# Last layer of a four-layer kernel: another hand order of its stages on all engines, and a rearranged opening

## The chip, the cores and the metric

One Trainium2 chip, one of its cores. The metric is the device time of one launch in microseconds (us). The time before is 2538.4 us, the median of three runs (2533.71 to 2541.52).

## What is computed

Four sub-layers run one after another on a batch of 2 sequences of 2048 tokens with 256 channels; each adds its result to its input. The change touches the last two, which the kernel does together. Per row of tokens, with `x` the sum of the layers so far:

```python
h = layernorm(x)                                   # without weights
xn = layernorm(h) * ln_w + ln_b
u, v, base = split(silu(xn @ uv_w.T + uv_b))       # 512, 512, 128 columns
q, k = rope(base * gamma[0] + beta[0]), rope(base * gamma[1] + beta[1])
kern = square(relu(q @ k.T / sqrt(128) + w[j - i + 127]))   # 2048 x 2048 for each sequence
y = x + (u * (kern @ v)) @ o_w.T + o_b + h
out = y + layernorm(y) @ (ternary(weight) * alpha) + d_bias
```

The kernel treats a whole sequence of 2048 tokens as the attention's length: 16 tiles of 128 keys by 4 chunks of 512 queries, for each of 2 sequences.

## The kernel before, in words

Layer functions `layer_a`, `layer_b` and `layer_c` run in turn, with all engines meeting between them. The change is in `layer_c` alone (from line 1787 on). It has two kinds of work.

**Steps.** There are 16 steps of 256 tokens (`n` from 0 to 15, eight for each sequence). In a step GpSimd (POOL) adds the two halves of the input (`sum`, L2016) when its rows have come by DMA (`load`, SyncE's queue, which waits until the sum before is done); VectorE (DVE) takes the moments (`moments`, L2150 to L2156); POOL takes the root (`moments`, L2020); DVE normalizes (`norm`, L2166); TensorE (PE) turns the rows (`turn_h`, L2342); ScalarE (ACT) and DVE split the result in a high and a low part (`turn_h`, L2076 and L2204), since each product is made of three matmuls (`product3`, lines L39 to L41). PE then makes `base` (6 matmuls of 256 columns), `u` in two halves (12 each) and `v` in two halves (7 of 512 columns each, the first one the bias, L2374). For `base`, ACT applies silu and scales (L2084 to L2093), DVE multiplies by the rotary table (L2211), POOL adds (L2033), and ACT and DVE split (`qk`, L2122 and L2222).

**Tiles.** There are 128 tiles (`i`). For each PE makes `scores` (3 matmuls of 512 columns), DVE turns them to `kern` in two instructions (L2232 reads the bank, L2236), ACT takes the high part (`high`, L2126), POOL the low part (`low`, L2037), and PE multiplies with `v` (`values`, 12 matmuls of 512 columns). After every 16 tiles a chunk is finished by stages that hang on later tiles (`after`): gate, project, residual, `turn_y`, `ternary`, `out`.

Steps 0 to 7 open the layer and overlap with tiles 0 to 9; steps 8 to 15 lie beside tiles 48 to 63. In the rest there are tiles alone.

**The order is written out by hand.** `order` names for each engine the stages of one slot and a shift; `turns` and `in_slots` unroll it. Each engine executes its own list strictly in that order, so an instruction that waits holds all that stand behind it in the list.

**PSUM banks.** `bank_uses` walks PE's list and gives each use the next bank: of all eight until the first `scores`, from then on of four (`narrow`: 0, 1, 2, 7) for everything but the outputs of `values`. A bank's next user waits on PE (`wait_bank`) until the engine that reads the last one has drained it. In the list before, with eight narrow uses to a slot, `turn_h(n+1)` follows a half of `u` in its bank; the bank of `scores` 2k is the one of `base`.

**Opening.** `shifts` on PE (20 records of one column, L2323, and 4 of 512 columns, L2328) makes the sums of the weights with `ln_b`; it is issued behind `turn_h` of step 0. DVE's `shifts` (L2180 to L2187) makes bias rows of them, which `base` on ACT and `v` on PE wait for. DVE's `weights` (L2173) makes the low part of the weights. After `v` (1, 1) PE makes `total` (L2335), one sum that DVE's `signs` (L2192 to L2200, after `qk` of step 1) waits for in its middle. `scores` of tile 0 need `q_lo_ready` of 2, that is `qk` of steps 0 and 1.

The two lists around the first steps, as the tables unroll them (numbers are step, or step and half, or tile):

```
PE before   turn_h0 [shifts] base0 u0,0 u0,1 v0,0 turn_h1 v0,1 base1 u1,0 u1,1 v1,0 turn_h2 v1,1 [total]
            base2 u2,0 u2,1 v2,0 scores0 turn_h3 scores1 v2,1 base3 u3,0 u3,1 v3,0 scores2 values0 turn_h4
DVE before  moments0 norm0 [weights] turn_h0 [shifts] moments1 norm1 base0 turn_h1 moments2 qk0 norm2 base1
            turn_h2 moments3 qk1 [signs] norm3 base2 turn_h3 kern0 kern1 v0,0 moments4 qk2 norm4 base3
```

Of the kernel before, what the change touches and what calls it, by code (L numbers as in the profile page):

```python
# [10 lines left out]
ALU = mybir.AluOpType  # L11
ACT = mybir.ActivationFunctionType
# [4 lines left out]
KC = D // P  # L17
# [1769 lines left out]
def layer_c(nc, io, psum, sem, early):  # L1787
# [9 lines left out]
    narrow, outputs = (0, 1, 2, 7), (3, 4, 5, 6)  # L1797

    order = {
        "act": [("v", 1, 2), ("base", 0, 3), ("u", 0, 3), ("after", 0, 4), ("high", 1, 3), ("u", 1, 3), ("turn_h", 0, 4),  # L1800
                ("v", 0, 3), ("high", 0, 4), ("qk", 0, 3), ("after", 1, 4)],
        "pe": [("u", 0, 3), ("u", 1, 3), ("after", 1, 2), ("v", 0, 3), ("scores", 0, 4), ("values", 0, 3),
               ("turn_h", 0, 4), ("scores", 1, 4), ("values", 1, 3), ("after", 0, 3), ("v", 1, 3), ("base", 0, 4)],
        "dve": [("norm", 0, 5), ("base", 0, 4), ("v", 1, 1), ("after", 0, 5), ("turn_h", 0, 5), ("kern", 0, 5),
                ("kern", 1, 5), ("v", 0, 2), ("moments", 0, 6), ("qk", 0, 4), ("after", 1, 5)],
        "sp": [("tile", 1, -1), ("tile", 0, 0), ("store_u", 0, 0), ("load", 0, 4), ("residual", 0, 1), ("rope", 0, 1)],
        "pool": [("after", 0, 7), ("sum", 0, 8), ("base", 0, 6), ("residual", 0, 7), ("low", 0, 7), ("after", 1, 7),
                 ("moments", 0, 8), ("low", 1, 7)],
    }
    of_tiles = ("values", "scores", "kern", "high", "low", "after", "tile")  # L1810
    halved = ("u", "v")
# [9 lines left out]

    def bank_uses():
        slot_banks = tuple(range(8))
        for name, slot, part in turns(order["pe"], slots):
            for at in places(name, part, slot):
                if name == "scores":
                    slot_banks = narrow
                if name == "values":
                    if at[0] % NT == 0:
                        for e in range(C_EC):  # L1830
                            yield ("o", (at[0] // NT, e)), outputs
                elif name == "after":
                    if NT <= at[0] and at[0] % NT in project_after:
                        stage, n = project_after[at[0] % NT]
                        yield (stage, (at[0] // NT - 1, n)), slot_banks
                else:
                    yield (name, at if name in halved else at[0]), slot_banks
                    if name == "turn_h" and at[0] == 0:
                        yield ("shifts", 0), slot_banks
                        yield ("shifts", 1), slot_banks  # L1840
                    if (name, at) == ("v", (1, 1)):
                        yield ("total", 0), slot_banks
        for stage, n in project_after.values():
            yield (stage, (C_TILES // NT - 1, n)), slot_banks

    with ExitStack() as ctx:
# [26 lines left out]
        x2 = [sb(f"x2{k}", [P, 2, D]) for k in range(2)]  # L1873
# [126 lines left out]
        @block.gpsimd  # L2000
        def _(pool):
            pool.memset(power[:], -0.5).then_inc(consts_ready, 1)
            pool.memset(ones[:], 1.0).then_inc(consts_ready, 1)
            pool.memset(e0[:].bitcast(F32), 0.0).then_inc(consts_ready, 1)
            pool.wait_ge(consts_ready, 3)
            pool.memset(e0[0:1, :].bitcast(F32), 1.0).then_inc(consts_ready, 1)
            pool.memset(e0[32:33, :].bitcast(F32), 1.0).then_inc(consts_ready, 1)
            pool.wait_ge(consts_ready, 5)

            def sum_(n):  # L2010
                if n > 0:
                    pool.wait_ge(x_loaded, 32 * n)
                if n > 1:
                    pool.wait_ge(xn_ready, n - 1)
                    pool.wait_ge(r_ready, n - 1)
                pool.tensor_tensor(x2[n % 2][:], x_in[:], y_in[:], ALU.add).then_inc(summed, 1)  # L2016

            def moments(n):
                pool.wait_ge(var_ready, n + 1)
                pool.tensor_tensor(rstd[:], var[:], power[:].rearrange("p (a b) -> p a b", a=2), ALU.pow).then_inc(rstd_ready, 1)  # L2020

            def residual(n):
                pool.wait_ge(xn_ready, n + 1)
                if n == 0:
                    pool.wait_ge(row_in, 80)
                r = r_out[n % 2]
                pool.tensor_tensor(r[:], x2[n % 2][:], r[:], ALU.add).then_inc(pool_own, 1)
                pool.wait_ge(pool_own, n + 1)
                pool.tensor_tensor(r[:], r[:], o_b[:, None, :].broadcast_to([P, 2, D]), ALU.add).then_inc(r_ready, 1)

            def base_(n):
                pool.wait_ge(rotated, n + 1)
                pool.tensor_tensor(turned[:, :, 0, :], turned[:, :, 0, :], turned[:, :, 1, :], ALU.add).then_inc(turned_ready, 1)  # L2033

            def low_part(i):
                pool.wait_ge(hi_ready, i + 1)
                pool.tensor_tensor(kern_lo[i % RING][:], kern[i % RING][:], kern_hi[i % RING][:].bitcast(F32), ALU.subtract)\  # L2037
                    .then_inc(lo_ready, 1)

            def add_bias(g):  # L2040
                pool.wait_ge(x3_ready, 2 * g + 2)
                if g > 0:
                    pool.wait_ge(stored, 16 * g)
                pool.tensor_tensor(x_out[:], x3[:], d_bias[:, None, :].broadcast_to([P, 4, D]), ALU.add).then_inc(biased, 1)

            def root(g):
                pool.wait_ge(y_var_ready, g + 1)
                pool.tensor_tensor(y_rstd[:], y_var[:], power[:], ALU.pow).then_inc(y_rstd_ready, 1)

            def after(i):  # L2050
                if i >= NT and i % NT == 5:
                    add_bias(i // NT - 1)
                if i >= NT and i % NT == 6:
                    root(i // NT - 1)

            in_slots(order["pool"], slots, places, {"low": low_part, "after": after, "base": base_, "moments": moments,
                                                    "residual": residual, "sum": sum_})
            root(C_TILES // NT - 1)
            add_bias(C_TILES // NT - 1)

        @block.scalar
        def _(act):
# [5 lines left out]
                act.activation(shift_rows[:, c, :], ones[:], ACT.Copy, scale=gb[:, 1, c:c + 1]).then_inc(rows_ready, 1)  # L2068
            for c in range(KC):
                act.activation(w_hi[:, c, :], w_raw[:, c, :], ACT.Copy, scale=gb[:, 0, c:c + 1]).then_inc(w_hi_ready, 1)  # L2070

            def turn_h(n):
                ring.wait_full(act, ("turn_h", n))
# [69 lines left out]
        def _(dve):  # L2143
            own = Links(dve, dve_own)
            dve.wait_ge(consts_ready, 5)

            def moments(n):
                dve.wait_ge(summed, n + 1)
                for w in range(2):
                    ins = dve.bn_stats(stats[:, w, :], x2[n % 2][:, w, :])  # L2150
                own.link(ins)
                for w in range(2):
                    ins = dve.bn_aggr(mv[:, w, :], stats[:, w, :])
                own.link(ins)
                dve.tensor_scalar(var[:, :, 0], mv[:, :, 1], EPS, None, ALU.add)
                dve.tensor_scalar(var[:, :, 1], mv[:, :, 1], 1.0 + EPS, EPS * EPS, ALU.mult, ALU.add).then_inc(var_ready, 1)  # L2156
# [156 lines left out]

        @block.tensor
        def _(pe):
            pe.wait_ge(consts_ready, 5)

            def shifts():
                pe.wait_ge(rows_ready, KC)
                ring.wait_bank(pe, ("shifts", 0))  # L2320
                for n, col in enumerate(list(range(0, C_E, P)) + [2 * C_E]):
                    for c in range(KC):
                        ins = pe.matmul(ring.out(("shifts", 0), C_EC + 1)[:, n:n + 1], w_raw[:, c, col:col + P], gb[:, 1, c:c + 1],  # L2323
                                        start=(c == 0), stop=(c == KC - 1))
                ring.written(ins, ("shifts", 0))
                ring.wait_bank(pe, ("shifts", 1))
                for c in range(KC):
                    ins = pe.matmul(ring.out(("shifts", 1), C_E), shift_rows[:, c, :], w_raw[:, c, C_E:2 * C_E],  # L2328
                                    start=(c == 0), stop=(c == KC - 1))
                ring.written(ins, ("shifts", 1))  # L2330

            def total_():
                pe.wait_ge(dve_setup, 1)
# [3 lines left out]
            def turn_h(n):  # L2337
# [4 lines left out]
                        ins = pe.transpose(ring.out(("turn_h", n), 512)[:, c * C_STEP + w * P:c * C_STEP + (w + 1) * P],  # L2342
                                           xn[:, w, c * P:(c + 1) * P], ident[:])
                ring.written(ins, ("turn_h", n))
                if n == 0:
                    shifts()

            def columns(n, job, part, col):
                for c in range(KC):
# [18 lines left out]
            def v(n, w):  # L2368
                at = n, w
                if n == 0 and w == 0:  # L2370
                    pe.wait_ge(b_ready, 4)
                ring.wait_bank(pe, ("v", at))
                tok = slice(w * P, (w + 1) * P)
                pe.matmul(ring.out(("v", at), C_E), e0[:], b_rows[:], start=True, stop=False)  # L2374
# [219 lines left out]
```

## Time and profile before

| | |
|---|---|
| profiled execution, whole | 2539.21 us |
| its span, first to last instruction | 2537.1 us |
| mean granted TensorE clock | 0.972 of full |
| PE busy | 2433.2 us (96%) |
| DVE busy | 1979.4 us (78%) |
| ACT busy | 1559.1 us (61%) |
| POOL busy | 1294.1 us (51%) |

The last layer opens at about 1856 us of the span and fills the 681 us that are left. All times below are microseconds from the start of the span. In timelines a row reads: start, time that it took (merged instructions together), engine, line, operation, output, input, shape, count; in brackets the idle time of the engine ahead of it and what ended it. A matmul's own time overlaps the next one's, so the step from start to start is what it costs.

### The profile page before, as it was taken

What the parts mean: (1) busy time and instruction counts of PE and PEld (TensorE: products, weight loads), DVE (VectorE), ACT (ScalarE), POOL (GpSimd) and SP (SyncE); (2) the same over time, 40 slices, a digit from 0 to 9 for tenths busy, and PEclk for the clock granted to TensorE, in tenths of its full rate; (3) what the DMA queues carried; (4) which work ended last, traced back from release to release, by engine and by line L of the source; (5) the groups of instructions that cost most, each with busy time, mean ns of one, the idle gap of its engine ahead of it and who ended that gap; (6) DMA issues with size and microseconds to landing.
All of it is one profiled execution on the core that took longest, in us unless ns stands there. A gap on an engine that the chain in (4) does not pass through costs nothing. (4 is left out here: it accounts for less than half of the span.)

```text
span 2537.1 us, 57174 instructions
## 1 busy us (share of the span) xinstructions
PE 2433.2 (96%) x20030; PEld 2203.1 (87%) x20030; DVE 1979.4 (78%) x6034; ACT 1559.1 (61%) x3626; POOL 1294.1 (51%) x1161
## 2 busy tenths in 40 slices
PE   7999999988999999999989999999879999999997
PEld 6999999977799999998989999999868888888886
DVE  6899999866888888988888898888557655775554
ACT  4788888754777777786867877877546213631111
POOL 2333333225766756767656566667246435743332
PEclk7999999997999999999999999999989999999998
DMA  2011221112222322323333223223242112311111
GB/s 79 21 33 37 71 87 58 42 49 74 88 76 91 98 74 87 101 78 111 111 95 97 80 86 101 76 87 95 94 154 90 38 42 85 107 63 34 34 34 42
DMA packets 223618, 190.21 MB, mean 75 GB/s; under 512 B 22372, under 2 KB 205800, under 8 KB 222312
## 3 DMA queue, kind: packets, MB, share of 16 engines
q1 hardware_dynamic: 204616, 176.91, 22.3%
q10 hardware_dynamic: 18720, 9.64, 1.3%
q8 instruction: 164, 2.69, 0.5%
q14 instruction: 118, 0.97, 0.1%
HBM read 91.00 MB, written 44.04 MB: 53 GB/s over the span
## 5 line engine op out<-in xcount | busy, mean ns | idle before, releaser
L1299 POOL TENSOR_TENSOR b_sb_probs<-b_sb_probs,b_sb_r_sum 128x512 f32<-128x512 f32 x256 | 269.0, 1073 | 350.8 <-DVE b_sb_r_sum L1532 350.8
L2037 POOL TENSOR_TENSOR c_kern_lo<-c_kern,c_kern_hi 128x512 fp32r<-128x512 f32 x128 | 178.4, 1394 | 302.7 <-ACT c_kern_hi L2126 302.7
L1383 ACT ACTIVATE b_sb_probs<-b_sb_probs,b_sb_neg_top,b_sb_r_norm 128x256 f32<-128x256 f32 x512 | 301.0, 590 | 7.1 <-DVE b_sb_neg_top L1511 6.3
L2126 ACT ACTIVATE c_kern_hi<-c_kern 128x512 fp32r<-128x512 f32 x128 | 80.9, 632 | 322.1 <-DVE c_kern L2236 322.1
L39 PE MATMUL psum<-b_sb_fT_lo,b_sb_w_hi 128*128 128x256 f32 x768 | 223.1, 290 | 2.2 <-DVE b_sb_fT_lo L1570 1.4
L41 PE MATMUL psum<-b_sb_fT_hi,b_sb_w_hi 128*128 128x256 f32 x768 | 217.5, 283 | 0.0
L40 PE MATMUL psum<-b_sb_fT_hi,b_sb_w_lo 128*128 128x256 f32 x768 | 217.3, 283 | 0.0
L1504 DVE CUSTOM_DVE_ANT_0 b_sb_probs<-psum,b_sb_mask 128x256 f32<-128x256 f32 x512 | 194.1, 415 | 7.8 <-PE psum L1675 7.7
L39 PE MATMUL psum<-c_kern_lo,c_v_hi 128*128 128x512 f32 x512 | 199.6, 390 | 0.1
L41 PE MATMUL psum<-c_kern_hi,c_v_hi 128*128 128x512 f32 x512 | 199.5, 390 | 0.0
L40 PE MATMUL psum<-c_kern_hi,c_v_lo 128*128 128x512 f32 x512 | 199.3, 389 | 0.0
L39 PE MATMUL psum<-b_sb_w_lo,b_sb_hT_hi 128*128 128x512 f32 x384 | 164.2, 428 | 1.1 <-DVE b_sb_hT_lo L1453 0.6
L522 ACT ACTIVATE a_probs<-a_probs,a_neg_top 128x128 f32<-128x128 f32 x512 | 157.1, 391 | 12.3 <-DVE a_neg_top L669 11.7
L2232 DVE SCALAR_TENSOR_TENSOR c_kern<-psum,c_bias 128x512 f32<-128x512 f32 x128 | 88.0, 687 | 95.2 <-PE psum L41 93.9
L41 PE MATMUL psum<-b_sb_w_hi,b_sb_hT_hi 128*128 128x512 f32 x384 | 152.6, 397 | 0.0
L40 PE MATMUL psum<-b_sb_w_hi,b_sb_hT_lo 128*128 128x512 f32 x384 | 151.0, 393 | 0.0
L39 PEld LDWEIGHTS psum<-b_sb_fT_lo,b_sb_w_hi 128*128 128x128 f32 x768 | 145.5, 189 | 5.3 <-DVE b_sb_fT_lo L1570 1.8
L40 PEld LDWEIGHTS psum<-b_sb_fT_hi,b_sb_w_lo 128*128 128x128 f32 x768 | 146.2, 190 | 2.6
L41 PEld LDWEIGHTS psum<-b_sb_fT_hi,b_sb_w_hi 128*128 128x128 f32 x768 | 145.8, 190 | 0.0
L1696 PE MATMUL psum<-c_ident,b_sb_probs 128*128 128x128 f32 x1024 | 135.2, 274 | 5.7 <-POOL b_sb_probs L1299 3.2
L1576 DVE SCALAR_TENSOR_TENSOR b_sb_mid<-psum,b_sb_b,b_sb_gate 128x256 f32<-128x256 f32 x192 | 92.2, 480 | 57.5 <-ACT b_sb_gate L1417 56.3
L1696 PEld LDWEIGHTS psum<-c_ident,b_sb_probs 128*128 128x128 f32 x1024 | 117.3, 141 | 17.8 <-POOL b_sb_probs L1299 5.1
(308 smaller groups left out, 8711.5 us busy)
## 6 DMA issues: line engine op xcount, KB each, us to landing
b_sb_v_prev<-b_sb_v_now SPq DMA_DIRECT2D x64, 256.0 KB, 3.6
b_sb_kT_hi<-b_sb_kT_hi SPq DMA_DIRECT2D x64, 256.0 KB, 3.3
b_sb_kT_lo<-b_sb_kT_lo SPq DMA_DIRECT2D x64, 256.0 KB, 3.7
Y<-b_sb_y SPq DMA_DIRECT2D x128, 128.0 KB, 1.9
b_sb_res<-Y SPq DMA_DIRECT2D x64, 128.0 KB, 2.1
b_sb_x_f<-Y SPq DMA_DIRECT2D x128, 64.0 KB, 2.0
b_sb_res_f<-Y SPq DMA_DIRECT2D x64, 128.0 KB, 2.2
U<-c_u_out SPq DMA_DIRECT2D x16, 512.0 KB, 4.6
```

Of the source, the lines that this page charges most:

```text
L39: pe.matmul(out, w_hi, x_lo, start=first, stop=False)
L40: pe.matmul(out, w_lo, x_hi, start=False, stop=False)
L41: return pe.matmul(out, w_hi, x_hi, start=False, stop=last)
L522: ins = act.activation(probs[b][:, h, :], probs[b][:, h, :], ACT.Exp, bias=neg_top[b][:, h:h + 1], scale=float(A_HD) ** -0.5)
L1299: pool.tensor_tensor(p, p, r_sum[b][:, 2 * m:2 * m + 2, None].broadcast_to([P, 2, 2 * P]), ALU.mult)\
L1383: ins = act.activation(probs[b][:, n, :], probs[b][:, n, :], ACT.Exp, bias=neg_top[b][:, n:n + 1], scale=r_norm[b][:, h:h + 1], accum_out= ...
L1504: ins = dve.tensor_tensor_reduce(out=probs[b][:, n, :], in0=ring.out(t, (f"s{m}", b), 512)[:, j * 256:(j + 1) * 256], in1=mask[:, min(t % ...
L1576: ring.read(t, dve.scalar_tensor_tensor(out=mid[m % 2][:], in0=ring.out(t, ("w", m), 512)[:, 256:512], scalar=b1[:, t // NT, 2 * m + 1:2 * ...
L1696: ins = pe.transpose(ring.out(t, (f"p{m}", b), 512)[:, i * P:(i + 1) * P], probs[b][:, n, half * P:(half + 1) * P], ident[:])
L2037: pool.tensor_tensor(kern_lo[i % RING][:], kern[i % RING][:], kern_hi[i % RING][:].bitcast(F32), ALU.subtract)\
L2126: act.activation(kern_hi[i % RING][:], kern[i % RING][:], ACT.Copy).then_inc(hi_ready, 1)
L2232: ring.read(dve.scalar_tensor_tensor(out=kern[i % RING][:], in0=ring.out(("scores", i), C_CHUNK), scalar=float(C_S) ** -0.5, in1=bias[:, a ...
```

## The change

1. The tables of `order` are new for all five engines. What they unroll to in the first steps (and with later numbers in steps 8 to 15):

```
PE after    [shifts] turn_h0 base0 u0,0 u0,1 turn_h1 v0,0 v0,1 base1 u1,0 u1,1 turn_h2 scores0 v1,0 v1,1 [total]
            scores1 base2 u2,0 u2,1 turn_h3 scores2 v2,0 v2,1 values0 scores3 base3 u3,0 u3,1 values1 turn_h4
            scores4 v3,0 v3,1 values2 scores5 base4 u4,0 u4,1 values3 turn_h5 scores6 ...
DVE after   moments0 norm0 [weights] moments1 turn_h0 [shifts] norm1 base0 moments2 turn_h1 qk0 v0,0 v0,1 norm2
            base1 moments3 turn_h2 qk1 [signs] kern0 v1,0 v1,1 norm3 base2 moments4 kern1 turn_h3 qk2 kern2 v2,0
            v2,1 norm4 base3 moments5 kern3 turn_h4 qk3 kern4 v3,0 v3,1 norm5 base4 moments6 kern5 turn_h5 ...
ACT after   ... v3,0 v3,1 high4 base4 u4,0 u4,1 high5 turn_h5 ...
POOL after  sum0 moments0 sum1 moments1 residual0 sum2 base0 moments2 residual1 sum3 base1 moments3 residual2 ...
```

In the stretches with tiles alone the order of `scores`, `values` and `kern` is as it was; the chunk stages on PE stand one `values` earlier. Since banks follow PE's list, the users of a bank are others too: `scores1` follows `scores0`, and `turn_h(n+1)` follows the odd-numbered `scores` of its slot (`turn_h3` `scores1`, `turn_h5` `scores5`); among steps 8 to 15 `turn_h9` follows `project`, `turn_h12` `turn_y`, `turn_h14` `ternary`.

2. PE issues `shifts` ahead of everything in the layer, without the wait for POOL's constants; its first part no longer waits for ACT's `rows_ready`.
3. The first sum of inputs is made on DVE.
4. ACT runs a silu of one column behind the weight split, so that the table is loaded there.

```diff
     def bank_uses():
         slot_banks = tuple(range(8))
+        yield ("shifts", 0), slot_banks
+        yield ("shifts", 1), slot_banks
...
-                    if name == "turn_h" and at[0] == 0:
-                        yield ("shifts", 0), slot_banks
-                        yield ("shifts", 1), slot_banks
...
             def sum_(n):
-                if n > 0:
-                    pool.wait_ge(x_loaded, 32 * n)
+                if n == 0:
+                    return
+                pool.wait_ge(x_loaded, 32 * n)
...
             for c in range(KC):
                 act.activation(w_hi[:, c, :], w_raw[:, c, :], ACT.Copy, scale=gb[:, 0, c:c + 1]).then_inc(w_hi_ready, 1)
+            act.activation(base[:, 0, 0:1], ones[:, 0:1], ACT.Silu)
...
             def moments(n):
+                if n == 0:
+                    dve.tensor_tensor(x2[0][:], x_in[:], y_in[:], ALU.add).then_inc(summed, 1)
                 dve.wait_ge(summed, n + 1)
...
-            pe.wait_ge(consts_ready, 5)
-
             def shifts():
-                pe.wait_ge(rows_ready, KC)
                 ring.wait_bank(pe, ("shifts", 0))
...
                 ring.written(ins, ("shifts", 0))
+                pe.wait_ge(rows_ready, KC)
                 ring.wait_bank(pe, ("shifts", 1))
...
                 ring.written(ins, ("shifts", 1))
+
+            shifts()
...
                 ring.written(ins, ("turn_h", n))
-                if n == 0:
-                    shifts()
...
                 if n == 0 and w == 0:
                     pe.wait_ge(b_ready, 4)
+                    pe.wait_ge(consts_ready, 5)
```

The tables for PE and DVE (shift last; a stage with a larger shift runs that many slots ahead):

```diff
-        "pe": [("u", 0, 3), ("u", 1, 3), ("after", 1, 2), ("v", 0, 3), ("scores", 0, 4), ("values", 0, 3),
-               ("turn_h", 0, 4), ("scores", 1, 4), ("values", 1, 3), ("after", 0, 3), ("v", 1, 3), ("base", 0, 4)],
+        "pe": [("values", 0, 0), ("scores", 1, 1), ("after", 0, 0), ("base", 0, 0), ("u", 0, 0), ("u", 1, 0), ("values", 1, 0),
+               ("turn_h", 0, 1), ("scores", 0, 2), ("after", 1, 0), ("v", 0, 0), ("v", 1, 0)],
-        "dve": [("norm", 0, 5), ("base", 0, 4), ("v", 1, 1), ("after", 0, 5), ("turn_h", 0, 5), ("kern", 0, 5),
-                ("kern", 1, 5), ("v", 0, 2), ("moments", 0, 6), ("qk", 0, 4), ("after", 1, 5)],
+        "dve": [("kern", 0, 1), ("after", 0, 1), ("v", 0, -1), ("v", 1, -1), ("norm", 0, 1), ("base", 0, 0), ("moments", 0, 2),
+                ("kern", 1, 1), ("after", 1, 1), ("turn_h", 0, 1), ("qk", 0, 0)],
```

## Rows read from the trace of the kernel before

**Rows 1.** Busy time by stretch: start:end, us, PE, PEld, DVE, ACT, POOL, PEclk, DMA, GB/s.
```profile
2000.00:2100.00 100.00, 99.85 (x459) 83.56 (x458) 57.32 (x88) 17.14 (x28) 37.34 (x29) 1.00 0.09 27
```

**Rows 2.** Timeline, PE, from the opening to the fourth turning.
```profile
1862.54 1.09 PE L2342 MATMUL psum<-c_ident,c_xn 128*128 128x128 f32 x4 [10.14 <-DVE c_r_out L2166]
...
1867.55 3.76 PE L2328 MATMUL psum<-c_w_raw,c_shift_rows 128*128 128x512 f32 x4
...
1878.38 0.66 PE L2342 MATMUL psum<-c_ident,c_xn 128*128 128x128 f32 x4 [1.79 <-DVE c_r_out L2166]
...
1880.51 0.33 PE L39 MATMUL psum<-c_hT_lo,c_w_hi 128*128 128x256 f32 x1
...
1884.09 0.39 PE L2374 MATMUL psum<-c_b_rows,c_e 128*128 128x512 f32 x1
...
1887.43 0.66 PE L2342 MATMUL psum<-c_ident,c_xn 128*128 128x128 f32 x4 [1.55 <-DVE c_r_out L2166]
...
1892.51 0.58 PE L2335 MATMUL psum<-c_total,c_ones 128*128 128x1 f32 x2 [2.78 <-DVE c_total L2192]
...
1901.50 0.60 PE L2342 MATMUL psum<-c_ident,c_xn 128*128 128x128 f32 x4
```

**Rows 3.** Timeline, DVE, opening.
```profile
1858.57 0.75 DVE L2150 BATCH_NORM_STATS2 c_stats<-c_x 128x6 f32<-128x256 f32 x2 [5.71 <-POOL c_x L2016]
...
1859.71 0.16 DVE L2156 TENSOR_SCALAR c_var<-c_mv 128x2 f32<-128x2 f32 x1
...
1864.97 0.68 DVE L2204 TENSOR_TENSOR c_hT_lo<-psum,c_hT_hi 128x512 fp32r<-128x512 f32 x1
1871.45 0.17 DVE L2180 TENSOR_TENSOR c_b_col<-psum,c_b_raw 128x5 f32<-128x5 f32 x1 [5.80 <-PE psum L2328]
...
1875.96 1.72 DVE L2166 TENSOR_SCALAR c_xn<-c_x,c_mv,c_rstd 128x256 f32<-128x256 f32 x2 [1.14 <-POOL c_rstd L2020]
...
1881.38 0.80 DVE L2155 TENSOR_SCALAR c_var<-c_mv 128x2 f32<-128x2 f32 x1
```

**Rows 4.** Timeline, POOL, opening.
```profile
1856.23 0.10 POOL L2002 MEMSET c_power<- 128x4 f32 x1 [12.54 <-POOLq L2515]
...
1867.03 1.27 POOL L2016 TENSOR_TENSOR c_x<-c_x_in,c_y_in 128x512 f32<-128x512 f32 x1 [6.06 <-DMA c_y_in<-Y]
```

**Rows 5.** Timeline, ACT: the table load, and silu and scaling of step 2.
```profile
1872.24 1.28 ACT L2084 ACT_TABLE_LOAD   x1 [7.99 <-PE psum L41]
...
1894.62 0.47 ACT L2084 ACTIVATE c_base<-psum,c_b_col 128x256 f32<-128x256 f32 x1 [3.03 <-PE psum L41]
...
1896.10 2.08 ACT L2093 ACTIVATE c_turned<-c_base,c_beta,c_gamma 128x256 f32<-128x256 f32 x4
```

**Rows 6.** Timeline, DVE: signs' end, base of step 2, kern of tile 0.
```profile
1895.75 0.69 DVE L2200 TENSOR_TENSOR c_w_sign<-c_above,c_below 128x512 fp32r<-128x512 f32 x1
...
1898.21 1.29 DVE L2211 TENSOR_TENSOR c_turned<-c_turned,c_rope 128x512 f32<-128x512 f32 x2 [0.35 <-ACT c_turned L2093]
...
1903.37 0.68 DVE L2232 SCALAR_TENSOR_TENSOR c_kern<-psum,c_bias 128x512 f32<-128x512 f32 x1
```

**Rows 7.** Busy time by stretch, as in rows 1: where the granted clock falls and rises.
```profile
1891.50:1892.00 0.50, 0.00 (x0) 0.00 (x0) 0.50 (x2) 0.09 (x1) 0.50 (x1) 0.93 1.07 379
...
1898.50:1899.00 0.50, 0.50 (x5) 0.50 (x5) 0.50 (x2) 0.39 (x2) 0.00 (x0) 0.74 0.99 350
```

**Rows 8.** Timeline, PE, beside steps 8 to 15.
```profile
2122.71 0.66 PE L2342 MATMUL psum<-c_ident,c_xn 128*128 128x128 f32 x4 [1.08 <-DVE c_r_out L2166]
...
2170.91 0.60 PE L2342 MATMUL psum<-c_ident,c_xn 128*128 128x128 f32 x4
...
2185.00 0.60 PE L2342 MATMUL psum<-c_ident,c_xn 128*128 128x128 f32 x4
...
2194.91 0.39 PE L39 MATMUL psum<-c_hT_lo,c_w_hi 128*128 128x256 f32 x1 [1.69 <-DVE c_yT_lo L2273]
...
2225.61 0.39 PE L39 MATMUL psum<-c_hT_lo,c_w_hi 128*128 128x256 f32 x1 [0.83 <-DVE c_x_out L2278]
```

More of the change, by code:

```diff
@@ L1799, in layer_c @@
     order = {
-        "act": [("v", 1, 2), ("base", 0, 3), ("u", 0, 3), ("after", 0, 4), ("high", 1, 3), ("u", 1, 3), ("turn_h", 0, 4),
-                ("v", 0, 3), ("high", 0, 4), ("qk", 0, 3), ("after", 1, 4)],
-        "pe": [("u", 0, 3), ("u", 1, 3), ("after", 1, 2), ("v", 0, 3), ("scores", 0, 4), ("values", 0, 3),
-               ("turn_h", 0, 4), ("scores", 1, 4), ("values", 1, 3), ("after", 0, 3), ("v", 1, 3), ("base", 0, 4)],
-        "dve": [("norm", 0, 5), ("base", 0, 4), ("v", 1, 1), ("after", 0, 5), ("turn_h", 0, 5), ("kern", 0, 5),
-                ("kern", 1, 5), ("v", 0, 2), ("moments", 0, 6), ("qk", 0, 4), ("after", 1, 5)],
-        "sp": [("tile", 1, -1), ("tile", 0, 0), ("store_u", 0, 0), ("load", 0, 4), ("residual", 0, 1), ("rope", 0, 1)],
-        "pool": [("after", 0, 7), ("sum", 0, 8), ("base", 0, 6), ("residual", 0, 7), ("low", 0, 7), ("after", 1, 7),
-                 ("moments", 0, 8), ("low", 1, 7)],
+        "act": [("v", 1, -1), ("high", 0, 1), ("after", 0, 1), ("base", 0, 0), ("u", 0, 0), ("u", 1, 0), ("high", 1, 1), ("after", 1, 1),
+                ("turn_h", 0, 1), ("qk", 0, 0), ("v", 0, 0)],
+        "pe": [("values", 0, 0), ("scores", 1, 1), ("after", 0, 0), ("base", 0, 0), ("u", 0, 0), ("u", 1, 0), ("values", 1, 0),
+               ("turn_h", 0, 1), ("scores", 0, 2), ("after", 1, 0), ("v", 0, 0), ("v", 1, 0)],
+        "dve": [("kern", 0, 1), ("after", 0, 1), ("v", 0, -1), ("v", 1, -1), ("norm", 0, 1), ("base", 0, 0), ("moments", 0, 2),
+                ("kern", 1, 1), ("after", 1, 1), ("turn_h", 0, 1), ("qk", 0, 0)],
+        "sp": [("rope", 0, 0), ("store_u", 0, 0), ("residual", 0, 1), ("load", 0, 4), ("tile", 0, 0), ("tile", 1, 0)],
+        "pool": [("low", 0, 1), ("after", 0, 1), ("base", 0, 0), ("moments", 0, 2), ("residual", 0, 1), ("sum", 0, 3), ("low", 1, 1),
+                 ("after", 1, 1)],
     }
```

## The prediction, made before the changed kernel was built or run

> **What bounds the kernel now.** I read busy time by stretch first, then PE's timeline where it isn't full. In the stretches with tiles alone PE is busy 99.85 of 100 us at the full granted clock [rows 1]: there the time is PE's work, and the change leaves that work and its order as they are. So only PE's idle time and its time at the lower clock can change, and both lie in the last layer's opening and beside steps 8 to 15.
>
> In the opening PE idles until 1862.54, then 1.79, 1.55 and 2.78 us [rows 2]. The clock is low from before the layer to the end of the shift sums at 1871.3 (1867.55 + 3.76), and again from 1892 to 1898.8, after the 2.78 us of idle [rows 7]. The reader should see two prices: idle time itself, and a low stretch of 6.8 us, which loses half of its length, 3.4 us. Beside steps 8 to 15 PE waits 1.08, 1.69 and 0.83 us [rows 8]. The last two are waits for a bank, not for data: the matmul at 2194.91 reads `hT`, but what releases it is DVE's read of `turn_y` in the same bank (`u` (12, 1) follows `turn_y`(2, 0) there). This row is the key to the new order: a bank's next user waits for a DVE instruction in DVE's own order.
>
> **Prices.** 30 matmuls of 256 columns (`base` and both `u`) take 1884.09 - 1880.51 = 3.58 us, 0.119 each [rows 2]; so `base` 0.7, `u` 2.8. A slot with two tiles takes 2185.00 - 2170.91 = 14.1 us [rows 8]; without `base` and `u`, and 0.4 for the turning, 10.1 us are left for 44 matmuls of 512 columns, 0.23 each: `values` 2.8, `scores` 0.7, both `v` 3.3. At the low clock all double. From the end of `base` on PE: ACT 0.3 later, then 1898.18 - 1894.62 = 3.56 [rows 5]; DVE's product 1.29 [rows 6]; DVE's moments 1859.87 - 1858.57 = 1.30 [rows 3]; the first instruction of `kern` 0.68 [rows 6], less what overlaps, and a handing-over of 0.1: about 7.2 us from `base` to the release of the bank of a `kern` that stands behind `base` and `moments` on DVE.
>
> **Part 1, shift sums ahead.** They start at about 1856.3, where POOL's first instruction stands [rows 4], not at 1863.6, and take the same 7.7 us (to 1871.3), so they end at 1864.2. ACT's rows are ready long before their second part. The turning of step 0 comes behind them, done at 1865.3 instead of 1863.6. Nobody needs it sooner, for the next item.
>
> **Part 2, first sum on DVE.** 128x512 with both inputs in SBUF is 0.69 on DVE (the row of `w_sign`) [rows 6]; with a start near 1857.2 moments begin at about 1857.9 instead of 1858.57 [rows 3]. It gains 0.6 us, hidden under the shift sums. The next load isn't sooner: SyncE issues it behind the layer's constants.
>
> **Part 3, table load.** It took 1.28 us [rows 5] between PE's `base` and silu; part of it lay beside DVE's bias rows, which silu also waits for, so 0.5 to 0.8 us go. The Trainium skill (ScalarE: Activation LUTs, "What ACT_TABLE_LOAD costs") gives about 2.66 us for a switch with its drain; by that, up to 1.4 us more would go; the row has only the load, 1.28, and decides here.
>
> **Part 4, the lists: first slots.** (a) On DVE `moments` 1 now stands ahead of `turn_h` 0. The rows of step 1 land only for POOL's sum at 1867.03 [rows 4], which ends at 1868.3; moments 1.3, then the low part 0.68 [rows 3]: `base` 0 starts at 1870.4 instead of 1871.3. So of 7 us of earlier shift sums 0.9 are left. PE idles 5 us ahead of it, and starts `base` at the low clock, where before it started just as the clock rose: 30 matmuls cost up to 3.5 us more. ACT has silu from 1872.0, DVE's bias rows being ready by then.
> (b) `scores0` now stands in the slot of step 1, and needs `qk` 1. By walking ACT, DVE and POOL in their lists: scaled 0 at 1875.5, both `v` of step 0 read at 1881.3, scaled 1 at 1884.8, DVE's product to 1886.2, POOL to 1887.5, ACT's split 1888.2, DVE's 1889.1. PE has turned step 2 at about 1885.0 and waits some 4 us, with `v` 1 queued behind. The clock falls as it did after 2.78 us.
> (c) `total` is behind these: near 1895.9 (1893.5 if the clock stays up). DVE waits for it inside `signs`, with `kern0` behind. From `total` to the end of `signs` it took 1896.44 - 1892.51 = 3.9 us [rows 2, 6]; 2.7 to 3.9 us, then 0.68 of `kern0` until `scores1`, its bank's next user, may start: at about 1899.3. PE idles about 3.4 us.
> (d) `scores1` and `base` 2 at the low clock end at 1901.9; `turn_h3` follows `scores1` in its bank, and `kern1` is behind `base` 2 and `moments` 4 on DVE: 7.2 us later, at 1909.2. PE has 2.8 to 5.1 us of `u` to fill that.
> Before, `turn_h3` started at 1901.50 [rows 2], having done `v` (2, 0) (1.6) but not `scores1` (0.7). With the same content the new order is at 1909.2 against 1900.6: +8.6 us, with bounds of 6 (clock up at (b) and (c)) and 10.5.
>
> **Part 5, the lists: steady slots.** In each slot of steps 3 to 6 PE does `base` n, `u`, `values`, `turn_h(n+1)`. Cover behind `base` is 2.8 + 2.8 = 5.6 us, the release of the bank comes after 7.2: a wait of 1.6 us in each of four, 6.4 in all, and 0.4 in step 7, which has no moments. Bounds of one wait: 1.0 (hand-overs hidden) and 2.3, if DVE's small instructions are held by POOL as in the row of 0.80 us, which takes 0.17 alone [rows 3]. The Trainium skill (SBUF — State Buffer, "SBUF: two separate sides") says that DVE and POOL share a pair of ports, held by one for a whole instruction; by that rule POOL's `base` sum, which starts as DVE goes on, holds the last moments, and the wait would be near the upper end; that agrees with the rows of 1.72 and 0.80 us [rows 3].
>
> **Part 6, steps 8 to 15.** The same slots. `turn_h10`, 11, 13 wait 1.6 each. `turn_h9` and 14 follow `project` and `ternary`, whose readers on DVE stand behind the whole `kern` too: 7.2 + 0.7 + 0.7 = 8.6, less 5.6: 3.0 each. `turn_h12` follows `turn_y`, read behind `kern`, ACT's high parts of both (0.6 each) and DVE's 0.7: about 9.9, so 4.3. `turn_h15` and the `scores` of step 15 0.4 each. Sum 15.9; the 3.6 us of before [rows 8] go: +12.3.
>
> **Clock.** Waits of 3 us or more (the one at `turn_h3` and three in part 6) should let it fall; each low stretch loses up to 3.4 us. Some of this overlaps with the next wait, and 1.6 us alone did not do it before (1.79 and 1.55 did not [rows 2], 2.78 did [rows 2, 7]). I take 6 us of at most 14, at least 0.
>
> **Sum.** 8.6 + 6.8 + 12.3 + 6 = 33.7 us. The profiled execution took 2539.2 us, 0.8 above the median of the three runs, 2538.4: 2539.2 + 33.7 less 0.8 gives 2572.1. Bounds: 6 + 4.5 + 8 + 0 = 18, 2557; 10.5 + 9.5 + 17 + 14 = 51, 2590.
>
> **Rivals.** *The slot's chain is shorter than its cover.* If ACT's and DVE's steps overlap more than their rows sum up to, or PE's records hide slack, the bank waits vanish; the opening stays at +6 to 10: 2546 to 2552. Against it: the same kind of wait is in the trace at 2194.91.
> *Nothing measurable.* The opening alone is half as dear and the waits of before (3.6 us, and 6.1 of idle) go: 2531 to 2546.
> *Faster.* The new lists feed PE throughout: 0.9 from the start, 6.1 us of idle and the low stretch of 3.4 us go, and 3.6 beside steps 8 to 15: 2538.4 - 14 = 2524. The point that decides is whether `scores0` finds `qk` 1 done when `turn_h2` is; it would take 4 us less on the chain over ACT, DVE, POOL, ACT and DVE. For it: both lists have the same work, and PE's steps of a slot stand closer together. Against: no term of that chain is shortened but the table load.
> By the Trainium skill (TensorE: Matmul & The Clock Gate, "HAM oscillation") a kernel whose gaps recur can drop to the low clock at each of them. If the ten waits of parts 5 and 6 all did so, 3.4 us each, it would be 2572 - 6 + 34 = 2600; the 1.79 and 1.55 us rows speak against it, and I give it a small chance.
>
> **Chances.** Forecast (2555 to 2592) 0.60; waits partly hidden, 2546 to 2555, 0.12; within 0.3% 0.11; faster 0.15; above 2592 0.02. 0.3%, 7.6 us, is about what a measurement of this kernel can tell from no change. The range 2540 to 2592 leaves out the faster case, the top and a part of the middle. Slower by over 0.3%: 0.74.
>
> **What the profile of after would show.** `base` 0 near 1870.4 at half clock; PE's wait at the first `scores` for DVE's `qk_lo` of about 4 us; a wait for `kern` at `scores1`; `turn_h` of most steps with 1 to 2.5 us of idle released by DVE's `kern`, at L2232; one of 4 us released by `yT_lo`; a row of lower PEclk in steps 8 to 15. If `turn_h` waits for nothing in steps 4 to 7, parts 5 and 6 are wrong; if `scores0` starts without a wait, part 4 is.

## The result, and the profile after

The changed kernel takes 2580.98 us (median of four runs), the one before 2539.96 us beside it: a ratio of 1.0162, 95% interval 1.0137 to 1.0187. The forecast of slower holds, and its time of 2572 us was 9 us short.

The profiled execution spans 2578.0 us, 40.9 more than before. Not all of that is the change: the last layer opens at 1858.10 here and at 1856.23 before (POOL's first instruction, as in [rows 4]), and all ahead of it is the same code. In the profiled executions of this study, one of each kernel, that point lay between 1849.65 and 1863.47. So I compare the layer from its own first instruction: 719.9 us against 680.9. The table below gives two sums over stretches of half a microsecond: TensorE's idle time, and its busy time multiplied by what the granted clock lacks to full.

| idle / lost to the low clock, us | before | after |
|---|---|---|
| first 60 us of the layer | 13.0 / 7.6 | 19.5 / 9.0 |
| next 70 us (steps 3 to 7) | 0.0 / 0.0 | 4.7 / 0.0 |
| tiles alone, to 255 us | 0.3 / 0.0 | 0.3 / 0.0 |
| steps 8 to 15, to 245 us before the end | 4.1 / 0.0 | 22.2 / 7.0 |
| last 245 us | 15.1 / 2.9 | 15.1 / 2.9 |

The differences add up to 37.7 of the 39.0 us. Nothing changed in the stretches with tiles alone, nor in the last one.

TensorE's timeline of the changed kernel shows the waits (columns as in [rows 2], which it answers); first the opening and the slots behind it:

```profile
1858.14 4.08 PE L2323 MATMUL psum<-c_gb,c_w_raw 128*128 128x1 f32 x20 [3.88 <-PEq L2517]
...
1872.07 0.58 PE L39 MATMUL psum<-c_hT_lo,c_w_hi 128*128 128x256 f32 x1 [5.98 <-DVE c_hT_lo L2207]
...
1887.74 0.66 PE L2345 MATMUL psum<-c_ident,c_xn 128*128 128x128 f32 x4 [2.19 <-DVE c_r_out L2169]
1891.67 0.80 PE L39 MATMUL psum<-c_qk_lo,c_qk_hi 128*128 128x512 f32 x1 [3.27 <-DVE c_qk_lo L2225]
...
1901.09 0.47 PE L39 MATMUL psum<-c_qk_lo,c_qk_hi 128*128 128x512 f32 x1 [3.10 <-DVE c_kern L2235]
1909.82 1.08 PE L2345 MATMUL psum<-c_ident,c_xn 128*128 128x128 f32 x4 [4.26 <-DVE c_kern L2235]
...
1927.14 0.63 PE L2345 MATMUL psum<-c_ident,c_xn 128*128 128x128 f32 x4 [1.52 <-DVE c_kern L2235]
```

The shift sums come first now. Then `base` of step 0 waits 5.98 us for the low part, the first `scores` 3.27 us for `qk` 1, `scores1` 3.10 us for its bank, `turn_h3` 4.26 and `turn_h4` 1.52 for theirs. The wait of 1.52 us returns at `turn_h5` and `turn_h6`. These are the places that the prediction named.

What holds the bank is read on DVE. `kern1` (L2235) stands behind the moments, and these behind DVE's product, which waits for ACT. The rows answer [rows 3, 6]:

```profile
1870.12 0.75 DVE L2153 BATCH_NORM_STATS2 c_stats<-c_x 128x6 f32<-128x256 f32 x2 [3.81 <-POOL c_x L2016]
...
1871.34 0.68 DVE L2207 TENSOR_TENSOR c_hT_lo<-psum,c_hT_hi 128x512 fp32r<-128x512 f32 x1
...
1898.10 0.16 DVE L2197 TENSOR_SCALAR c_delta<-psum 128x1 f32<-128x1 f32 x1 [5.89 <-PE psum L2338]
...
1900.26 0.69 DVE L2235 SCALAR_TENSOR_TENSOR c_kern<-psum,c_bias 128x512 f32<-128x512 f32 x1
...
1906.36 1.29 DVE L2214 TENSOR_TENSOR c_turned<-c_turned,c_rope 128x512 f32<-128x512 f32 x2 [1.20 <-ACT c_turned L2094]
1907.57 0.74 DVE L2153 BATCH_NORM_STATS2 c_stats<-c_x 128x6 f32<-128x256 f32 x2
...
1909.00 0.68 DVE L2235 SCALAR_TENSOR_TENSOR c_kern<-psum,c_bias 128x512 f32<-128x512 f32 x1
```

DVE itself is idle 3.81 us with `hT_lo` queued behind step 1's moments, and 5.89 us inside `signs` with `kern0` queued. `kern1` starts at 1909.00 and TensorE's turning 0.82 later.

Beside steps 8 to 15 the longest waits are not where I put them. TensorE's waits from 2100 to 2300 us (who waited for whom: us in total, times, longest):

```profile
PE psum L39 <- DVE c_kern L2235: 16.7, 3, 5.6
PE psum L2345 <- DVE c_kern L2235: 4.8, 3, 1.8
```

and one of the three on DVE's timeline and on TensorE's:

```profile
2153.53 1.29 DVE L2214 TENSOR_TENSOR c_turned<-c_turned,c_rope 128x512 f32<-128x512 f32 x2 [4.91 <-ACT c_turned L2094]
...
2156.17 0.68 DVE L2235 SCALAR_TENSOR_TENSOR c_kern<-psum,c_bias 128x512 f32<-128x512 f32 x1
```

```profile
2150.81 0.28 PE L39 MATMUL psum<-c_hT_lo,c_w_hi 128*128 128x256 f32 x1
...
2156.90 0.58 PE L39 MATMUL psum<-c_hT_lo,c_w_hi 128*128 128x256 f32 x1 [5.58 <-DVE c_kern L2235]
```

That is `u` (8, 1). `project` stands between the `scores` and `base` in this slot and takes a bank, so the second half of `u`, not the turning, is the next user of the odd `scores`' bank. It has only one half of `u` as cover: 1.4 us instead of 5.6. The same holds for `u` (11, 1), behind `turn_y`, and `u` (13, 1), behind `ternary`. The clock falls to half in each of the three, near 2155.6, 2213.6 and 2251.1 us; by stretch, for the first of them (columns as in [rows 1]):

```profile
2152.00:2156.00 4.00, 0.00 (x0) 0.00 (x0) 2.41 (x7) 2.21 (x6) 1.10 (x1) 0.93 0.05 6
2156.00:2160.00 4.00, 3.10 (x13) 3.06 (x14) 2.14 (x5) 0.13 (x1) 3.75 (x4) 0.50 0.19 59
```

### The profile page after: what moved, and what is told of

Same layout as the page of the kernel before. It is cut to its first block and busy times, and to the rows that moved or that the text cites. A ratio compares the mean times of both kernels' runs of the same rounds, so it can differ in the third digit from the quotient of the medians.

```text
span 2578.0 us, 57175 instructions
## 1 busy us (share of the span) xinstructions
PE 2443.2 (95%) x20030; PEld 2209.1 (86%) x20030; DVE 1994.1 (77%) x6035; ACT 1561.0 (61%) x3627; POOL 1283.1 (50%) x1160
## 5 line engine op out<-in xcount | busy, mean ns | idle before, releaser
L2037 POOL TENSOR_TENSOR c_kern_lo<-c_kern,c_kern_hi 128x512 fp32r<-128x512 f32 x128 | 172.6, 1350 | 289.9 <-ACT c_kern_hi L2127 289.9
L2235 DVE SCALAR_TENSOR_TENSOR c_kern<-psum,c_bias 128x512 f32<-128x512 f32 x128 | 87.9, 687 | 123.0 <-PE psum L41 122.5
```

The lines of the kernel that those rows point to most:

```text
L2235: ring.read(dve.scalar_tensor_tensor(out=kern[i % RING][:], in0=ring.out(("scores", i), C_CHUNK), scalar=float(C_S) ** -0.5, in1=bias[:, a ...
```

## Experiments

The theory: the new lists put the odd `kern` behind `base` and `moments` on DVE, and the bank order hands its bank to a stage that TensorE reaches sooner; a smaller part comes from the opening's lists; the three edits of the opening (shift sums first, first sum on DVE, table load early) cost nothing. The rivals: the three edits cost it; or the waits come from how close TensorE's own stages stand.

### Tables alone, and opening alone

`a1_tables_only` is the kernel before with the new `order`. `a2_opening_only` is the changed kernel with the old one:

```diff
-        "dve": [("kern", 0, 1), ("after", 0, 1), ("v", 0, -1), ...      # and the other four lists
+        "dve": [("norm", 0, 5), ("base", 0, 4), ("v", 1, 1), ...
```

> The kernel before with the new order tables alone; shift sums, first sum and table load stay where they were. Theory (the lists and the banks that follow from them cost the time): about as slow as the changed kernel, 2576 to 2583 us; base of step 0 starts right behind the shift sums at the full clock, so up to 3 us less than the changed kernel. Rival (the three edits of the opening cost it): near the kernel before, 2540, and the bank waits of 1.5 and 5.6 us on PE absent.

> The changed kernel with the old order tables: shift sums first, first sum on DVE, table load early. With the old lists nothing of step 1 stands ahead of the low part of step 0 on DVE, so base of step 0 can start 4 us sooner, though at the low clock. Theory: 1 to 6 us faster than the kernel before (2534 to 2539), and no bank waits by kern. Rival (the opening's edits are what costs): over 10 us slower than before.

Measured: tables alone 2583.10 us, ratio 1.0187 (1.0172 to 1.0202), at the upper end of what was expected and not below the changed kernel. The reason given for less time did not hold: `base` of step 0 started at the low clock here too, which rose only at 1872.3. It starts at 1869.70; by stretch (columns as in [rows 1]):

```profile
1870.50:1871.50 1.00, 1.00 (x6) 1.00 (x6) 0.87 (x2) 0.04 (x1) 0.92 (x2) 0.50 1.08 431
```

The low clock cost 13.5 us in the first 60 us of the layer, against 9.0 in the changed kernel. That difference can't be put down to the missing edits: `e1_kern_first_late` below has the changed kernel's lists and edits in all of this stretch and lost 15.3 us to the low clock and 15.9 to idle time, against 9.0 and 19.5. So a sum of both over one execution's opening is uncertain by some 3 us. Opening alone 2535.63 us against 2534.78, ratio 1.0000 (0.9981 to 1.0019). So the tables carry the whole loss, and the first rival falls. The opening's edits bring nothing that can be told in the whole time. The theory's 1 to 6 us of gain for them are not confirmed; in the layer's own length they show as 2.6 us (678.3 against 680.9) of one execution each. On TensorE with the old tables:

```profile
1864.19 0.38 PE L39 MATMUL psum<-c_hT_lo,c_w_hi 128*128 128x256 f32 x1 [1.41 <-DVE c_hT_lo L2207]
1873.03 1.12 PE L2345 MATMUL psum<-c_ident,c_xn 128*128 128x128 f32 x4 [3.40 <-DVE c_r_out L2169]
...
1889.47 0.38 PE L2338 MATMUL psum<-c_total,c_ones 128*128 128x1 f32 x2 [4.13 <-DVE c_total L2195]
```

`base` of step 0 starts 9.6 us into the layer (1864.19 less 1854.57) instead of some 15 (where the shift sums end before, 1871.3 [rows 2]), but the next waits grow from 1.79 and 2.78 us [rows 2] to 3.40 and 4.13. Most of the time saved was handed to the next waits. The first of them ends with the work on the rows of step 1, and these came by DMA at nearly the same point, 10.4 us into the layer (10.8 before, [rows 4]):

```profile
1864.94 1.59 POOL L2016 TENSOR_TENSOR c_x<-c_x_in,c_y_in 128x512 f32<-128x512 f32 x1 [6.24 <-DMA c_y_in<-Y]
```

### The odd kern ahead of base on DVE

```diff
-        "dve": [("kern", 0, 1), ("after", 0, 1), ("v", 0, -1), ("v", 1, -1), ("norm", 0, 1), ("base", 0, 0), ("moments", 0, 2),
-                ("kern", 1, 1), ("after", 1, 1), ("turn_h", 0, 1), ("qk", 0, 0)],
+        "dve": [("kern", 0, 1), ("after", 0, 1), ("v", 0, -1), ("v", 1, -1), ("norm", 0, 1), ("kern", 1, 1), ("after", 1, 1),
+                ("base", 0, 0), ("moments", 0, 2), ("turn_h", 0, 1), ("qk", 0, 0)],
```

> The changed kernel with one move on DVE: the odd-numbered kern of a slot and the chunk stage behind it stand ahead of base and moments instead of behind them; banks and all other lists are as in the changed kernel. Theory: the bank is released before base is even done on PE, all waits for kern in the slots go, also the 4.3 us at the turning of step 3, and the low clock beside steps 8 to 15: 28 to 36 us less than the changed kernel, 2545 to 2553. Rival (the waits come from the closeness of PE's own stages, whatever DVE's order): under 8 us gained.

Measured: 2551.99 us, ratio to before 1.0059 (1.0038 to 1.0079); 29 us less than the changed kernel by the medians, at the lower end of the expected 28 to 36. The two were run beside different groups of runs of before; by the ratios, 1.0162 less 1.0059, it is some 26 us, and the layer is 28.0 us shorter (691.9). No wait of TensorE is left from 1904 to 2133 us, and from 2100 to 2320 these are:

```profile
PE psum L39 <- DVE c_kern L2235: 5.3, 2, 4.0
PE psum L39 <- DVE c_u_in L2246: 2.7, 1, 2.7
```

Idle beside steps 8 to 15 fell from 22.2 to 8.7 us, the loss to the clock there from 7.0 to 3.0, and the 4.7 us of steps 3 to 7 went. The same banks and the same list on TensorE, so the second rival falls too.

`e1_kern_first_late` makes this move beside steps 8 to 15 only:

```diff
+            for i in range(-2, slots + 1):
+                for name, part, shift in order["dve"] if i < 24 else late:     # late: the list above
```

> The changed kernel with the odd kern ahead of base and moments on DVE only beside steps 8 to 15; steps 0 to 7 keep the changed kernel's list. Theory (the 22 us of idle and 7 us of low clock there are this one order): idle there falls to 8.7 and the low-clock loss to 3, as in the kernel with the move everywhere: 17 us less than the changed kernel, 2562 to 2566; the waits of 1.52 us and of 4.3 us in steps 2 to 6 stay. Rival (the gain of the full move came mainly from the opening, where it starts a better phase): under 9 us gained.

Measured: 2559.98 us, ratio to before 1.0091 (1.0078 to 1.0105). Idle beside steps 8 to 15 is 8.6 and the low-clock loss 3.2, as with the full move, and the waits of 1.52 us in steps 3 to 5 are all there. The wait at `turn_h3`, expected at 4.3, was 2.74 us, with more of the low clock around it; the layer is 15.3 us shorter (704.6), the 17.4 saved beside steps 8 to 15 less what this execution's opening lost more. The changed kernel's 1.0162 less 1.0091 is 0.7%, some 18 us; this one order of two stages is nearly half of the loss. The medians differ by 21 us, since each was run beside a different group of runs of before.

### Same lists, other banks

```diff
                 if name == "scores":
-                    slot_banks = narrow
+                    slot_banks, score_banks = (2, 7), (0, 1)     # chunk stages take score_banks too
```

> The changed kernel with the same lists on every engine and other banks: scores and the chunk stages take banks 0 and 1, steps take 2 and 7, so no stage of a step follows a scores in its bank. Theory (banks released by a kern that stands behind base and moments on DVE): the six waits of 1.5, the three of 5.6 and the one of 4.3 us go or fall under 1 us each, and the low clock beside steps 8 to 15 with them: 25 to 33 us less than the changed kernel, 2548 to 2556. Rival (PE waits in these slots for data that DVE's list makes late, and the bank is only named by chance): PE waits as long at the same places for other releasers, less than 8 us gained.

Measured: 2573.23 us, ratio 1.0148 (1.0130 to 1.0166), 8 us less than the changed kernel by the medians and 5.4 by the layer's length, with intervals that overlap: the theory's 25 to 33 us are missed, at the rival's number. What took their place:

```profile
1930.16 0.50 PE L2376 MATMUL psum<-c_b_rows,c_e 128*128 128x512 f32 x1 [0.91 <-DVE c_hT_lo L2207]
...
2201.84 0.50 PE L2376 MATMUL psum<-c_b_rows,c_e 128*128 128x512 f32 x1 [3.83 <-DVE c_hT_lo L2207]
```

The waits for `kern` are gone (three of 0.6 us are left), but with two banks for six stages of a step `v` (n, 1) follows `turn_h(n+1)`, whose reader on DVE stands behind the odd `kern`, and so behind `base` and `moments` as well. The change of banks has a price of its own besides. Idle time and low clock together fell by 12.6 us (68.1 against 80.7 in the whole layer), and the layer only by 5.4. With tiles alone the first `project` matmul of a chunk now comes 65.5 us behind that of the chunk before, instead of 64.6, some 5 us over the six chunks; that `scores` has two banks instead of four there would explain it, but isn't shown. So this was not a clean test: it changed which bank is late, not the list that makes it late. With the move on DVE it agrees that the list is the cause and the bank order the way by which it reaches TensorE.

### The opening's lists, one by one

Moments of step 1 behind the low part and bias rows of step 0:

```diff
             def turn_h_(n):
                 turn_h(n)
                 if n == 0:
                     shifts()
+                    moments(1)               # and not at its own place
```

> The changed kernel with one move: the moments of step 1 stand behind the low part and the bias rows of step 0 on DVE, as in the kernel before. Theory (the low part of step 0 was held for the rows of step 1): PE waits 2 us instead of 6 ahead of base of step 0, silu comes 3 us sooner; the first scores wait for a chain that starts from step 1's rows, so only a part arrives at the end: 1 to 4 us less than the changed kernel, 2577 to 2580. Rival (the wait for step 1's rows costs nothing, since the next waits absorb it): within 1 us of the changed kernel.

Measured: 2577.60 us, ratio 1.0147 (1.0132 to 1.0162), not told apart from the changed kernel's 1.0162. The medians differ by 3.4 us, which is in the theory's range, but the layer is no shorter, 720.8 against 719.9. So the rival fits better. The timeline shows where the gain went:

```profile
1862.77 0.38 PE L39 MATMUL psum<-c_hT_lo,c_w_hi 128*128 128x256 f32 x1 [1.41 <-DVE c_hT_lo L2207]
1872.50 1.11 PE L2350 MATMUL psum<-c_ident,c_xn 128*128 128x128 f32 x4 [5.94 <-DVE c_r_out L2169]
1887.81 0.79 PE L39 MATMUL psum<-c_qk_lo,c_qk_hi 128*128 128x512 f32 x1 [4.62 <-DVE c_qk_lo L2225]
```

5.98 us of wait at `base` became 1.41, and the turning of step 1 now waits 5.94 where it waited 0.67, `scores0` 4.62 where it waited 3.27, and the 2.19 us at the turning of step 2 are gone: 4.57 us less at `base`, and 4.43 more in all at the three places behind it.

`scores` of tile 0 behind `v` (1, 1):

```diff
                 if at == (1, 1):
+                    scores(0)
                     total_()
```

> The changed kernel with scores of tile 0 behind v (1, 1) instead of ahead of v (1, 0) on PE. Theory (scores0 waits 3.3 us for qk of step 1 with v queued behind, and total, signs, kern0 and scores1 follow late): the 3.3 us go, total comes 5 us sooner, scores1 follows v in its bank and waits for nothing, u (2, 0) may wait 2 us for kern0: 4 to 9 us less than the changed kernel, 2572 to 2577. Rival (the chain over base, moments and kern1 sets the turning of step 3 whatever stands ahead): under 2 us.

Measured: 2573.60 us, ratio 1.0128 (1.0108 to 1.0149). By medians 7 us less than the changed kernel, as the theory has it, but the intervals overlap, and by the layer's length it is 3.5 (716.4). Idle in the first 60 us fell by 6.3 us, but the low clock cost 3.8 more. The wait for `qk_lo` and the one at `scores1` are gone; `u` (2, 0) waits 2.48 us for `kern0`, as expected, and `turn_h3` 3.72.

`signs` and `total` one step later (their small tiles in memory of their own):

```diff
-                if n == 1:
+                if n == 2:
                     signs()
-                if at == (1, 1):
+                if at == (2, 1):
                     total_()
```

> The changed kernel with DVE's signs and PE's total one step later (behind qk of step 2 and v (2, 1)); their three small tiles get memory of their own, since kern of tile 0 would overwrite them. Theory (DVE is held inside signs for total, with kern of tile 0 behind, and scores1 waits for its bank): the wait of 3.1 us at scores1 goes, and DVE's 5.9 us of idle move; 2 to 5 us less than the changed kernel, less if DVE's new place holds kern of tile 2. Rival (signs' place doesn't matter): within 1 us.

Measured: 2573.17 us, ratio 1.0129 (1.0113 to 1.0145): 7.8 us less by the medians, more than expected, with intervals that overlap; the layer is 716.5, 3.4 us shorter, inside the expected 2 to 5 (one execution each, and near the 3 us by which two openings with the same lists differ). The 3.10 us at `scores1` are gone from TensorE's waits, the 3.27 at `scores0` and 4.35 at `turn_h3` stay. This fits the theory that `kern0` sat behind `signs`.

Three moves together (the odd `kern`, the moments of step 1, `scores0`):

> The changed kernel with three moves together: odd kern ahead of base and moments on DVE, moments of step 1 behind the low part of step 0, scores0 behind v (1, 1). Theory: 29 us as measured for the first, 2 and 6 for the others: 2540 to 2547, within 0.4% of the kernel before. Rival (what the single moves save overlaps): 2548 to 2552.

Measured: 2546.21 us, ratio 1.0030 (1.0017 to 1.0044), the upper end of what the theory gave. The new tables with three places mended are still no better than the old ones. In the profiled execution the opening is level with before (13.5 us of idle and 6.0 of low clock against 13.0 and 7.6); what is left stands beside steps 8 to 15, 8.6 and 3.4 against 4.1 and 0.0.

### Is there a version that beats both?

The old tables leave one wait in the opening that grew, the 4.13 us at `total`. The reduction for it made earlier, with the opening's edits and without:

```diff
+            def reduce_early():              # called behind the low part of step 1
+                dve.wait_ge(later_in, 64)
+                setup.link(dve.tensor_reduce(total[:], d_w[:], AX.XY, ALU.add, apply_absolute_value=True))
```

> The opening's edits with the old tables, and DVE's reduction for total made behind the low part of step 1, not behind qk of step 1. Theory (PE's 4.1 us of idle at total with the old tables are a wait for this reduction alone, and the low clock follows from it): 4 us of idle and up to 3.4 us at the low clock go: 5 to 8 us less than the kernel before, 2529 to 2534. Rival (PE then waits at the next stage for the normalization of step 3 instead): under 2 us.

> The kernel before with only the earlier reduction for total. Theory: 2.8 us of idle and 3.4 us at the low clock go, 4 to 6 us less than before, 2533 to 2536; what it lacks against the kernel with the opening's edits too, if anything, is what those edits bring once total is out of the way, 0 to 3 us. Rival: the next wait takes it, under 2 us.

Measured: 2534.82 us, ratio 0.9993 (0.9979 to 1.0006), and 2535.61 us, ratio 1.0000 (0.9991 to 1.0010). Neither can be told from the kernel before, so both expected gains, 5 to 8 and 4 to 6 us, were missed. The waits at `total` are gone in both; the turning of step 3 waits instead (1.41 and 1.14 us, where it waited for nothing). The layer of the first is 675.5 us long, 5.4 less than before, of the second 679.0, one execution each; a gain of that size is not shown in the whole time, where the layers ahead vary by more.

## Why the prediction was right, and where its terms were off

**What bounds it** held: with tiles alone nothing moved, and 37.7 of the 39.0 us are TensorE's idle time and low clock in the two places named and in the slots of steps 3 to 7 that part 5 has.

**Parts 1 to 3.** The shift sums took the place behind the layer's first instruction (the first one at 1858.14), the sum on DVE 0.69 us, the table load its 1.28 us behind the weight split (ACT's timeline):

```profile
1862.98 1.28 ACT L2071 ACT_TABLE_LOAD   x1
1864.27 0.20 ACT L2071 ACTIVATE c_base<-c_ones 128x1 f32<-128x1 f32 x1
```

The load costs 1.28 us with nothing else behind it but the 0.20 of the silu, which starts 0.01 after; the 2.66 us with a drain of the Trainium skill (ScalarE: Activation LUTs, "What ACT_TABLE_LOAD costs") don't show here. How much of it goes ahead of the first silu of `base`, put at 0.5 to 0.8 us, no run isolates.

**Part 4.** Counted from the layer's first instruction, `turn_h3` is 51.7 us in (1909.82 less 1858.10), before 45.3 [rows 2, 4]: 6.4 and the 0.9 of content, 7.4 us against 8.6 predicted. The waits were 3.27, 3.10 and 4.26 for the "some 4", "about 3.4" and 2 to 4 of the text. The chain from the end of `base` 2 to the turning was 7.24 us (1902.58 to 1909.82), as priced; what was mis-sized is the clock ahead of it. I had `scores1` and `base` 2 at the low clock, ending 45.7 us in; they ran at the full clock (1.00 in the row below) and ended 44.5 in, and that is the 1.2 us.

```profile
1901.50:1905.50 4.00, 4.00 (x33) 3.76 (x31) 3.65 (x7) 3.30 (x7) 1.61 (x1) 1.00 0.00 0
```

This was the luck of one execution: five kernels have the same wait of 3.10 us at `scores1`, and in three of their executions the clock fell in it or just behind it. And the 5.98 us ahead of `base` 0 were not worth mending: with 4.6 of them gone the layer was as long as before. The walk itself said so, since it let `scores0` hang on step 1's rows, and the 3.5 us that (a) names for starting `base` at the low clock stand in no term of the sum.

**Part 5.** One wait was put at 1.6 and measured 1.52, three times. The fourth (`turn_h7`) and the 0.4 us of step 7 are absent: in the slot of step 6 there are no moments, as step 8 comes much later. I had seen that for step 7 only. 4.6 us instead of 6.8. The row of the small DVE instruction beside POOL's `base` sum is 0.38 to 0.42 us here, not 0.80; alone it is 0.17. Ahead of `kern1` the two end together (1908.63 and 0.38 on DVE's timeline, 1907.73 and 1.26 on POOL's). That agrees with the lock that the Trainium skill describes (SBUF — State Buffer, "SBUF: two separate sides"). It adds some 0.2 us, so the upper end was not reached.

**Part 6 failed in place and size.** I had the bank table of these slots, and looked only at the turnings. Three waits of 3.0, 4.3 and 3.0 us at `turn_h9`, 12 and 14 were three of 5.58 us at `u` (8, 1), (11, 1) and (13, 1), which the chain of 7.2 us less 1.4 of cover would have given: 5.8. TensorE's idle rose by 18.1 us against 12.3. The `kern` of `scores` is released before the turning then, so nothing waits there. The three ordinary waits, put at 1.6, were 1.52, 1.76 and 1.52. What was released late was the same; who comes next in the bank was read too coarsely.

**Clock.** 6 us were taken, at most 14; it was 7.0 beside steps 8 to 15 and 1.4 in the opening. It fell in each of the three waits of 5.58 and in none of those of 1.5. In between the rows of all kernels differ: the wait of 3.10 us at `scores1` left the clock full in the changed kernel and in the run with the moments of step 1 moved, and fell in or just behind it in tables alone, with the odd `kern` moved everywhere and with it moved late. The rule of the Trainium skill (TensorE: Matmul & The Clock Gate, "HAM oscillation"), that recurring gaps can bring the low clock back each time, holds for the long ones alone here, 5.58 us against 1.52. So the rival of 2600 us falls.

**Sum.** 7.4 for the opening with its clock, 4.7 in steps 3 to 7, 18.1 of idle and 7.0 of low clock beside steps 8 to 15 are 37.2 us, where 33.7 had been predicted (8.6, 6.8, 12.3 and 6); the layer's length grew by 39.0, and the 1.8 us between are in no term of mine. The step that made the forecast short is part 6, by 6 us, which the opening and steps 3 to 7 made good in part (1.2 and 2.1 us less than predicted). Of the 9 us by which the time was missed another 1.6 are the kernel before, 2539.96 beside this one and 2538.4 when the forecast was made. The rivals: "chain shorter than its cover" falls with the 1.52 us; "nothing measurable" with the 41 us; "faster" falls at its own point, since `scores0` did not find `qk` 1 done.

## What to carry to other kernels

When an order by hand is changed, write down for each shared buffer who has it next and who must let it go, and compare the cover of the first with the whole queue ahead of the second on its engine: 7.2 us of chain against 5.6 or 1.4 of cover gave 1.52 and 5.58 us here, where the differences are 1.6 and 5.8. Do it for every user, also where an extra stage shifts the rotation by one, for that is where the dearest wait stood. And moving early work out of this opening paid only up to the next input that has a time of its own: taking 4.6 us away ahead of `base` changed the three waits behind it by 4.4 in all (5.27 and 1.35 more, 2.19 less), and in the old order some 5.5 us of earlier start came to nothing measurable in the whole time, and to 2.6 us of the layer's length.

## What the runs showed that I had not expected

The layers ahead of the change, the same instructions in each kernel, end between 1849.65 and 1863.47 us, a spread of 14 us or 0.5% of the span; the stretches with tiles alone are much steadier (0.3 to 0.4 us of idle in all kernels but the one with other banks). A difference of a few us in a late stage is better read from that stage's own start, as long as it is called one execution.

The opening's low clock is not steady. The changed kernel and `e1_kern_first_late` have the same lists up to step 8, yet in the first 60 us of the layer one lost 9.0 us to the low clock and the other 15.3, with 19.5 and 15.9 us of idle. So the exchange seen when `scores0` moved behind `v` (6.3 us less idle, 3.8 more at the low clock), in one execution, isn't shown to come from the move: its part at the low clock is within that spread.
